# Two up products of the first shared sequence stand in the last sequence's third head group, in two banks left by row scores

## The reference

```python
x = x + attention(layernorm(x))        # 16 heads of 8 channels, softmax over 512 keys
x = x + moe(layernorm(x))

def moe(x):                            # 8 experts, 2 of them per token, and one shared expert
    shared = gelu(x @ Wfc_s + bfc_s) @ Wproj_s + bproj_s          # 128 -> 512 -> 128
    gate   = the two largest softmax(x @ Wr), divided by their sum
    routed = sum over the two chosen experts of gate * (gelu(x @ Wfc[e] + bfc[e]) @ Wproj[e] + bproj[e])
    return shared + routed
```

## Time and profile before

| | us |
|---|---|
| median of 3 runs (all: 605.32, 605.17, 602.15) | 605.17 |
| span of the profiled execution, first to last instruction | 600.2 |
| PE busy / DVE busy / ACT busy / POOL busy in the span | 585.2 / 497.1 / 452.8 / 280.1 |

### The profile page before, as it was taken

One profiled execution on the slowest core, in us unless ns is written; L12 is line 12 of the kernel. 1 busy time (PEld: TensorE's weight loads), 2 busy tenths in 40 slices (PEclk: granted clock), 3 DMA queues, 4 the chain that ended last, 5 costly groups with the idle time before them and its releaser, 6 DMA issues.

```text
span 600.2 us, 21750 instructions
## 1 busy us (share of the span) xinstructions
PE 585.2 (98%) x8258; PEld 405.9 (68%) x8258; DVE 497.1 (83%) x1076; ACT 452.8 (75%) x967; POOL 280.1 (47%) x481
## 2 busy tenths in 40 slices
PE   6898999999999999999999999999999999999997
PEld 3443556555665655655655765656899999999966
DVE  8989999999999999999999999735577777777557
ACT  5887898888888888888888888985266555555551
POOL 7947430222542542542642642656745555555500
PEclk9999999999999999999999999999999999999999
DMA  6896333324434322322322311001422222222173
GB/s 177 224 303 208 110 80 93 102 79 121 126 91 128 90 57 61 85 57 64 82 57 66 82 56 47 21 20 49 93 56 67 70 70 70 71 70 70 42 294 136
DMA packets 43839, 57.66 MB, mean 96 GB/s; under 512 B 11130, under 2 KB 31482, under 8 KB 43754
## 3 DMA queue, kind: packets, MB, share of 16 engines
q1 hardware_dynamic: 39434, 47.59, 28.1%
q0 software_dynamic: 4320, 8.89, 4.6%
HBM read 35.76 MB, written 20.42 MB: 94 GB/s over the span
## 4 chain that ended last, share of the span: by engine, by line
PE 91%; ACT 3%; SPq 2%; DMA 1%; DVE 1%; issue 1%; POOL 0%; DVEq 0%; ACTq 0%
PE ps L1423 18%; PE ps L1451 18%; PE ps L1466 18%; PE ps L1677 11%; PE ps L1665 11%; PE ps L1624 4%; PE ps L1615 4%; PE ps L1405 2%; PE ps L1655 1%; PE ps L1486 1%; ACT xn L761 1%; PE ps L1411 1%; ACT probs L774 1%; PE ps L1497 1%; ACT probs L865 1%
## 5 line engine op out<-in xcount | busy, mean ns | idle before, releaser
L1002 DVE TENSOR_REDUCE mx<-ps 128x2 f32<-128x1024 f32 x256 | 306.2, 1212 | 20.2 <-PE ps L1423 12.2
L865 ACT ACTIVATE probs<-ps 128x512 f32<-128x512 f32 x512 | 296.8, 603 | 31.5 <-PE ps L1451 13.0
L1451 PE MATMUL ps<-q_op,k_op 128*32 128x512 bf16 x2048 | 205.0, 380 | 3.0 <-DMA q_op<-mxT 2.9
L1423 PE MATMUL ps<-k_op,q_op 96*32 96x512 bf16 x2048 | 161.0, 380 | 1.8 <-DVE mx L1002 1.3
L1466 PE MATMUL ps<-probs,v_op 128*32 128x256 f32 x2048 | 160.0, 378 | 0.0
L923 ACT ACTIVATE probs<-ps,b_cur 128x128 f32<-128x128 f32 x284 | 80.8, 368 | 59.4 <-PE ps L1665 58.6
L739 POOL DMA_INDIRECT results<-rest,row_id x71 | 71.6, 1009 | 66.5 <-DVE rest L1303 48.0
L1423 PEld LDWEIGHTS ps<-k_op,q_op 96*32 96x32 bf16 x2048 | 62.1, 97 | 52.9 <-DVE mx L1002 14.2
L1466 PEld LDWEIGHTS ps<-probs,v_op 128*32 128x32 f32 x2048 | 70.9, 109 | 38.7 <-ACT probs L865 0.2
L1451 PEld LDWEIGHTS ps<-q_op,k_op 128*32 128x32 bf16 x2048 | 64.5, 95 | 46.4 <-ACT probs L865 3.1
L630 POOL DMA_INDIRECT slots<-route_sb,slot_u x64 | 63.7, 995 | 58.0 <-ACT probs L865 49.7
(11 more groups left out here) (177 smaller groups left out, 543.0 us busy)
## 6 DMA issues: line engine op xcount, KB each, us to landing
q_op<-q_scr SPq DMA_DIRECT2D x96, 96.0 KB
k_op<-k_scr SPq DMA_DIRECT2D x96, 96.0 KB
w_sb<-in_W SPq DMA_DIRECT2D x18, 256.0 KB, 3.0
probs<-slots SPq DMA_DIRECT2D x71, 64.5 KB, 1.8
q_scr<-probs SPq DMA_DIRECT2D x8, 384.0 KB, 3.8
k_scr<-probs SPq DMA_DIRECT2D x8, 384.0 KB, 3.7
k_scr<-probs SPq DMA_DIRECT2D x8, 256.0 KB, 4.4
probs<-results SPq DMA_DIRECT2D x4, 512.0 KB, 4.8
```

The source lines that it names most:

```text
L865: nc.scalar.activation(probs[:, i, j, :], ps[:, BANK["key", b, hg, s], :], ACT.Exp, scale=float(D) ** -0.5).then_inc(s_exp, 1)
L1002: nc.vector.reduce_max(mx[:, slot % 2, 2 * p:2 * p + 2], ps[:, bank:bank + 2, :], AX.X).then_inc(s_max, 1)
L1423: last = nc.tensor.matmul(ps[c, BK_A + a % 4, :], q_op[hg][0:SH, j, P * i + c.start:P * i + c.stop], k_op[hg][0:SH, j, :], start=True, sto ...
L1451: last = nc.tensor.matmul(ps[c, bank, :], k_op[hg][:, j, P * i + c.start:P * i + c.stop], q_op[hg][:, j, :], start=True, stop=True)
```

## The change

`up(0, (0,))` and `up(0, (1,))` move from behind the last pv into steps 5 and 8 of the third head group of the last sequence, and write banks 4 and 5 in place of 0 and 1. Behind the last pv the orders of PE and of ACT are written anew.

```diff
+        FIRST_UP_AT, FIRST_UP_BANKS = ((HG - 2, 5), (HG - 2, 8)), (4, 5, 2, 3)
+        def up_bank(b, c):
+            return FIRST_UP_BANKS[c] if b == 0 else UP0 + c
# ACT
-                nc.scalar.activation(hid[:, b % 2, c, :], ps[:, UP0 + c, :], ACT.Gelu_apprx_tanh,
+                nc.scalar.activation(hid[:, b % 2, c, :], ps[:, up_bank(b, c), :], ACT.Gelu_apprx_tanh,
             gelus(0)
-            gelu(1, 0)
-            gelu(1, 1)
+            gelus(1)
             for i in range(NT // 2):
                 ln2_normalise(B - 1, i)
-            gelu(1, 2)
-            gelu(1, 3)
             copy_yT(B - 1)
# PE
+            def up(b, chunks=range(FC)):
+                for c in chunks:
+                    if b > 1 or b == 1 and up_bank(0, c) == up_bank(1, c):
+                        wait(pe, s_gelu, (b - 1) * FC + c + 1)
+                    if c == 0:
+                        pe.wait_ge(s_yT, b + 1)
+                    nc.tensor.matmul(ps[:, up_bank(b, c), :], w1_sb[:, E, P * c:P * (c + 1)], yT[:, b, :],
+                                     start=True, stop=True).then_inc(s_up, 1)
             def attend(b):
...
+                        if last_b and (hg, s) in FIRST_UP_AT:
+                            pe.wait_ge(s_wffn, 16 * N_WFFN)
+                            pe.wait_ge(s_max, NG * J * NT // 2)
+                            up(0, (FIRST_UP_AT.index((hg, s)),))
...
-            up(0, range(FC - 1))
+            up(0, (2, 3))
+            up(1, (0,))
             project_out(B - 1)
-            up(0, (FC - 1,))
-            up(1)
-            down(0, (0,))
+            up(1, (1, 2, 3))
+            down(0, (0, 1))
             transpose_y(B - 1)
-            down(0, (1,))
+            down(0, (2,))
             router(B - 1)
-            down(0, (2,))
+            down(0, (3,))
             up(2, (0,))
             ranks(B - 1)
-            down(0, (3,))
             pe.wait_ge(s_cn, (B + 1) * Q)
```

More of the change, by code:

```diff
@@ L1608, in _ @@
             pe.wait_ge(s_rkc, B - 1)
[L1610 to L1616, removed]
             def down(b, tiles=range(NT)):
```

## The result

The changed kernel takes 605.79 us (median of 9 runs, 603.96 to 607.88), the kernel before in the same measurement 602.70 (9 runs, 602.00 to 605.32). The ratio is 1.0036 with a 95% interval of 1.0020 to 1.0053: slower by 2.2 us (1.2 to 3.2). 2.2 us is less than the half percent (3.0 us) named in the prediction, though the interval just reaches it, and it leaves no room for a gain: 1.72 us of work were taken out of a busy tail, and the kernel is slower.

A forecast was written before the change was run, and what follows sets the result against it. The prediction took PE to bound the third group, but for one short wait, and the tiles, with the routing chain pacing the tail. +2.14 - 0.54 - 0.28 - 0.15 = +1.2 us on 605.17 gave 606.4 us, range 602.8 to 609.0.

The forecast's parts named there:

- two products in the group: Third head group: each moved product takes 1.07 us, switches of array mode included, +2.14 us for the two.
- bank waits displaced: Third head group: PE's waits for a bank at the keys of steps 10 and 11 disappear, -0.54 us.
- copy of yT sooner: Tail: with two gelus moved ahead of the normalisation, ACT's copy starts after less delay, chain -0.28 us.
- count product sooner: Tail, behind the ranks: with no down tile there, the count product starts with the running counts, -0.15 us.
- loads of tiles: Start of the tiles: loads move by 1.32 us, PE by 1.17, so 0.25 us of slack stays, no cost.
- the upper bound of the sum: Whole kernel: +2.4 us, with the dearest switch and no gain at the copy and the counts.
- Part 1: Third head group: what the two moved products cost there, 2.14 us, between 1.72 without a switch price and 2.5.
- Part 2: Third head group: only 0.54 us of bank waits hides the products; new waits cost nothing; last pv 1.60 us later.
- Part 3: Tail: the routing chain sets the pace, 1.72 us less work returns as idle 1.0 and 0.8; tiles +1.17 us.
- (a): Rival, third head group: ACT alone bounds it, the products are free, 604.7 us; chance 0.10.
- (b): Rival, tail: it is PE's alone, 1.72 us less work and no idle, 603.5 us; chance 0.08.
- (c): Rival, tail: two new idle stretches bring the clock down, 610.3 us with 4 us of work at half speed; chance 0.05.

The follow-up runs named there:

- e6: The changed kernel with ACT's gelus 2 and 3 of sequence 1 back between the normalisation and the copy of yT; 605.40 us, ratio 1.0020.
- e2: The changed kernel run once more with no edit; 606.48 us, ratio 1.0046.
- e3: The changed kernel with each of the two moved products cut into four matmuls of 32 columns; 605.44 us, ratio 1.0032.
- e4: The changed kernel with the two moved products computing only 16 of their 512 columns each; 604.61 us, ratio 1.0015.
- e8: The changed kernel with each moved product computed twice in its place; 608.69 us, ratio 1.0084.
- e9: The changed kernel with up(2, (1, 2)) directly behind the ranks, ahead of the count product; 626.68 us against 625.33, ratio 1.0023.
- e12: The changed kernel with one product moved, to step 9, in 32 columns, and up(2, (1, 2)) behind the ranks; 626.20 us against 625.33, ratio 1.0015.
- e10: The kernel before with only the count product moved, ahead of the fourth down tile, directly behind the ranks; 624.53 us against 625.33, ratio 0.9990.
- e11: The changed kernel with SP's padding reads and filling rows started two table steps later; 625.77 us against 625.33, ratio 1.0009.
- e7: The changed kernel with only the first product moved, to step 9 of the third group, and PE's tail reordered; 605.00 us, ratio 1.0010.
- e1: The kernel before run once more as a control, no edit; 603.10 us, ratio 1.0007.

## Why the prediction was right, and where it was not

The sign held, and so did the mechanism up to the tiles: the products are paid for in the group, and the tail gives nothing back. The size is nearly twice the forecast, +1.2 us against +2.2 and +2.8 in two measurements and +2.27 in the profiles. The difference stayed under half a percent, as forecast, but half a percent was not "about what a measurement of this kernel can tell": both measurements of the change tell it from nothing. Term by term, in us, counted from t3:

| term | predicted | measured |
|---|---|---|
| two products in the group | +2.14 | +2.38 (2 x 1.19) |
| bank waits displaced | -0.54 | -0.49 (2.38 less 1.89) |
| so far: last pv | +1.60 | +1.89 |
| copy of yT sooner | -0.28 | about 0: taken by DVE's wait for the puts (e6) |
| count product sooner | -0.15 | -0.18, or +0.02 in e2, where y came 0.23 later |
| so far: PE reaches the tiles | +1.17 | +1.71, or +1.92 in e2 |
| loads of tiles | 0, slack 0.25 | +0.5, or +0.3 in e2 |
| sum: second transposes of tiles | +1.17 | +2.2 |

**Two pieces of luck.** The forecast time, 606.4 us, lies close to the measured 605.79 because it was built on the median of three runs, 605.17, while that of nine is 602.70; from there +1.2 gives 603.9. And the upper bound of the sum, +2.4, counts the gains at the copy and the counts twice. With the dearest switch and neither gain it is 2.5 - 0.54 = +2.0, and +2.27 lies above that: the loads, which the sum has at nothing, are what took it there.

**Part 1** undersized the switch: 0.21 us per product from the transposes, 0.33 from the profile after and 0.30 in e3. Ahead of the product it is much the same (0.14, 0.11 for the transposes), behind it more (0.19 against 0.10). Why is not shown; the number of columns does not explain it, since 16 columns pay no less (e4). Without the switch the group would take the 9.65 of e3.

**Part 2** held: its 0.54 us of bank waits are 0.49, nothing else in the group gives (e8), and the waits for row maximum and weights cost nothing (e3).

**Part 3** had the mechanism, two idle stretches of 1.0 and 0.8 us (0.85 and 0.91), which is why 1.72 us less work gained nothing there. Two steps of it failed. The first is "With those gelus moved ahead of the normalisation, where ACT lies idle, the copy starts 0.28 us after less delay: chain -0.28": the copy does start sooner, the chain doesn't move, because the slots have a second parent, POOL's puts of the sequence before, that was tied with it. The second is "POOL's puts come by the same shift" and with it "so 0.25 stays": the first put comes 1.84 us later from t3, and the eight then take 1.07 us longer from first to last issue, so that the loads become the bound of the tiles' start. That shorter puts alone would bring the tiles forward is argued from this chain and not shown: the two changed kernels with shorter puts, e9 and e12, are the ones with the late gelus. One of the prediction's own signs of being wrong, "tiles that wait for their loads, in which case POOL's puts are the bound", thus came true.

What slows the puts is the phase of DVE's table steps, which follow the count product, against them: e9 and e12 hold the product back and have 9.31, e10 brings it forward in the kernel before and has 10.10, and e11 clears SP's rows. No run moves DVE's steps by themselves, but the rows of all 14 profiles, 8 puts each, agree. Each of the 61 puts that are longer than 1.05 us starts while DVE is in a table step that reads two operands in SBUF (34 of them) or in a copy of weights from SBUF to SBUF (27), with 0.21 to 0.54 us of it left, and is longer than 0.96 by what is left less some 0.1. The other 51 start with 0.06 us of such a step left at most, and are 0.95 to 1.04 long; steps of other kinds, a reduction or an addition out of PSUM, leave a put at 0.96 with up to 0.7 us of theirs left.

**The rivals.** (a), the group hides the products: out by the group's +1.89 and by e8. (b), the tail is PE's: out by the two idle rows, and e7 agrees. (c), the clock: the windows from 402 to 435 are at 1.00 in the changed kernel, so it played no part. e9 shows that it can, after 0.82 and 1.36 us of idle PE, and e12 that it need not, after 0.98 and 1.19.

## What to carry to other kernels

An engine that is busy all through a stretch can still be filler around a chain: before taking work out of it, walk the chain with the work removed and see what idle time appears, and count every parent of its steps, ties too. Work moved into a stretch of another array mode pays for both switches, and costs what it displaces only as far as a wait is really there; cutting it to the mode around it (four matmuls of 32 columns) took the price of the switch away here, though the kernel with it (e3) was still slower than before. Measure a small change from a mark just ahead of it, not by whole spans: here the start of the kernel scattered by up to 2.8 us, more than the change costs.

## What the runs showed of the hardware

- A product 128x512 float32 of full width between matmuls of 32 columns takes 1.19 us (the profile after), tiled it takes 0.86 (e3), and 16 columns of full width take 0.47 (e4). The Trainium skill (TensorEngine Tiling (Array Packing), Key Properties) says that a change of mode drains the engine. The time lost at both ends agrees with that rule, which comes without a price; the runs give 0.3 us.
- POOL's indirect writes of 128 rows take 0.95 to 0.98 us of POOL each, and up to 1.38 where they start while DVE is in a step with two operands in SBUF or in a copy from SBUF to SBUF: the rest of that step less some 0.1 us is added. A phase of 0.07 or 0.08 us decides (the step L1254 starts at 417.42 and the write at 417.35 before; the same step, L1256, at 419.54 and the write at 419.62 in e2). The Trainium skill (SBUF — State Buffer, SBUF: two separate sides) says that VectorE and GpSimd share a pair of ports by an exclusive lock that an operation of VectorE with two inputs in SBUF takes too, against one of GpSimd that reads SBUF. The lengthened writes fit that. The other way round no row shows a wait: the step L1254 takes 0.41 us in the first profile, where a write is under way as it starts, and 0.41 us in the changed kernel, where it starts ahead of the write.
- The granted clock fell to its lower level for a few microseconds within the first 60 us in some executions of both kernels, among them the profiles of the changed kernel and of e1, in which the third group started 1.5 and 1.3 us later than in the first profile.
- Two idle stretches of PE close to each other brought the granted clock to its lower level in e9 (0.82 and 1.36 us, 1.17 of work between) and left it at 1.00 in e12 (0.98 and 1.19, 1.39 between). Single ones of 0.85 and 0.91 us, some 5 us apart, left it at 1.00 in the changed kernel.
